# Row scatters of a mixture-of-experts layer spread singly over GpSimd's order

## What is computed

```python
x = x + tanh(g_xattn[0]) * cross_attention(ctx_2048, layernorm(x), mask, mask, ...)   # 8 heads of 16
x_flat = layernorm(x).reshape(-1, 128)
scores = sigmoid(x_flat @ gate.T + bias)                  # 2048 tokens x 9 experts
top_scores, selected = top_k(scores, 2)
top_scores = top_scores / (sum(top_scores) + 1e-20)
for e in range(9):
    h = silu(x_flat @ ew1[e].T) * (x_flat @ ew3[e].T)     # hidden width 352
    out = out + cw[:, e:e + 1] * (h @ ew2[e].T)           # cw: the weight of expert e, or 0
x = x + tanh(g_ffn[0]) * out
```

## Time and profile before

| | |
|---|---|
| timed, median of 3 (lowest, highest) | 231.89 us (231.73, 232.34) |
| profiled execution: span from first to last instruction | 242.9 us |
| profiled execution: its own time around the span | not recorded |
| mean granted TensorE clock of the profiled execution | 0.942 of 2.4 GHz |
| PE, ACT, DVE, POOL busy, share of the span | 83%, 59%, 57%, 51% |
| POOL: x_rows scatters L554, 32 | 32.3 us, 1011 ns mean |
| POOL: y_rows scatters L572, 40 | 39.6 us, 989 ns mean |

### The profile page before, as it was taken

How to read it: one execution, slowest core, us unless ns; L and a number is a source line. 1 busy time by engine, 2 the same in 40 slices (tenths; PEclk the granted TensorE clock), 3 DMA queues, 4 the chain that set the end, 5 groups by cost and what they waited for, 6 DMA issues and landing times.

```text
span 242.9 us, 5743 instructions
## 1 busy us (share of the span) xinstructions
PE 200.9 (83%) x1530; PEld 158.7 (65%) x1531; DVE 139.5 (57%) x511; ACT 143.5 (59%) x400; POOL 123.4 (51%) x209
## 2 busy tenths in 40 slices
PE   8989896999989998977858980599999999999200
PEld 2667653667656665654637870599999999998200
DVE  0397896688897678976643953133444443444035
ACT  0556969788778866875427630356666666665100
POOL 4228735132335784775683477345555555555500
PEclk9999998899999999999988998589999999999955
DMA  5999999987000100011364121112222121260085
GB/s 129 312 331 384 399 402 402 393 304 283 0 4 12 36 33 11 25 34 37 77 167 127 48 66 55 33 46 65 71 67 54 41 58 51 61 213 26 0 299 219
DMA packets 21946, 32.65 MB, mean 134 GB/s; under 512 B 3345, under 2 KB 14742, under 8 KB 21794
## 3 DMA queue, kind: packets, MB, share of 16 engines
q1 hardware_dynamic: 18082, 27.59, 33.7%
q0 software_dynamic: 2304, 4.24, 5.3%
q10 hardware_dynamic: 1536, 0.54, 0.9%
HBM read 15.77 MB, written 17.10 MB: 135 GB/s over the span
## 4 chain that ended last, share of the span: by engine, by line
PE 59%; DVE 14%; issue 10%; DMA 6%; ACT 6%; POOL 2%; ACTq 1%; another core or an unknown queue 0%; POOLq 0%; DVEq 0%; SPq 0%
PE pt_ps L1193 11%; PE score_ps L1155 7%; PE score_ps L1157 5%; PE score_ps L1156 5%; PE pt_ps L1202 5%; PE score_ps L1013 4%; DMA xs<-in_x 4%; PE ps_a L1063 4%; PE ps_b L1118 3%; PE pt_ps L1051 3%; DVE xs L971 2%; PE ps_b L1120 2%; PE ps_a L1172 2%; DMA kheads<-y_rows 2%; DVE less L763 2%
## 5 line engine op out<-in xcount | busy, mean ns | idle before, releaser
L572 POOL DMA_INDIRECT y_rows<-probsT,ids x40 | 39.6, 989 | 32.3 <-ACT probsT L458 24.4
L1193 PE MATMUL pt_ps<-w,probsT 128*128 x234 | 34.7, 287 | 9.6 <-issue 9.2
L1193 PEld LDWEIGHTS pt_ps<-w,probsT 128*128 128x128 f32 x234 | 32.3, 201 | 10.7 <-issue 10.1
L390 ACT ACTIVATE probs<-score_ps,less 128x128 f32<-128x128 f32 x128 | 37.5, 405 | 0.4 <-DVE less L763 0.4
L554 POOL DMA_INDIRECT x_rows<-stage,slot x32 | 32.3, 1011 | 8.8 <-issue 8.8
L914 DVE TENSOR_TENSOR xg_low<-ps_a,xg_high 128x128 fp32r<-128x128 f32 x40 | 11.7, 291 | 43.5 <-ACT xg_high L443 37.0
L458 ACT ACTIVATE probsT<-pt_ps,xg 128x128 f32<-128x128 f32 x39 | 14.3, 367 | 33.5 <-PE pt_ps L1193 27.4
L1155 PE MATMUL score_ps<-w_high,xg_low 128*128 x80 | 30.2, 377 | 0.2
L921 DVE TENSOR_TENSOR probs<-probs,score_ps 128x352 f32<-128x352 f32 x40 | 20.8, 520 | 14.7 <-PE score_ps L1157 5.7
L1156 PE MATMUL score_ps<-w_low,xg_high 128*128 x80 | 26.5, 331 | 0.0
L1157 PE MATMUL score_ps<-w_high,xg_high 128*128 x80 | 26.5, 331 | 0.0
(11 more groups left out here) (152 smaller groups left out, 415.2 us busy)
## 6 DMA issues: line engine op xcount, KB each, us to landing
x_rows<-pads SPq DMA_DIRECT2D x1, 9945.0 KB, 36.5
w_low<-in_w13T SPq DMA_DIRECT2D x3, 1056.0 KB, 10.8
xg<-x_rows SPq DMA_DIRECT2D x40, 65.0 KB, 1.8
ctx_r<-in_ctxT SPq DMA_DIRECT2D x4, 512.0 KB, 8.7
w<-in_w2T SPq DMA_DIRECT2D x1, 1728.0 KB, 9.0
kheads<-y_rows SPq DMA_DIRECT2D x3, 512.0 KB, 4.9
mask_b<-in_mask SPq DMA_DIRECT2D x4, 256.0 KB, 9.0
out<-xs SPq DMA_DIRECT2D x1, 1024.0 KB
```

Source lines behind the costliest of these rows:

```text
L390: last = nc.scalar.activation(probs[:, r % 2, h, :], score_ps[:, r % 2, h, :], ACT.Exp, bias=less[:, r % 2, h:h + 1])
L572: pool.indirect_dma_start(y_rows[:, :], bass.IndirectOffsetOnAxis(ap=ids[:, r:r + 1], axis=0), yt[:, r, :], None, bounds_check=last_row, o ...
L1193: last = nc.tensor.matmul(into[:, 0:D], hidT[:, q3, c, :], w2[:, bass.ds(e3, 1), c, :].rearrange("p o d -> p (o d)"), start=(c == 0), stop ...
```

## The change

It moves scatters; their number and size stay.

- In attention, a group's four batches go out in four steps, one a step: group 0 in steps 9 to 12, group 1 in steps 13 to 16. Of a batch's two scatters the first stands between `rstd2_of` and `keep`, the second at the step's end; `v_cur` moves from the step's start to behind `keep`.
- Behind the last step, batches 0 and 1 of group 2 stand singly between the norms of batches 14 and 15. Batches 2 and 3, and all of group 3 (now in one row behind tile 3), are `paced`: each scatter waits until the last but one has landed.
- Each scatter place has a semaphore of its own, counted to 16 a group; SyncE waits for 8 of them instead of 4 before a row of tile loads, `weigh` too, and `norm2` for 2 instead of 1.

```diff
-        st_rows = [sem(f"st_rows{n}") for n in range(UN)]
+        st_rows = [sem(f"st_rows{n}") for n in range(2 * UN)]
...
-        st_last = [sem(f"st_last{n}") for n in range(UN)]
+        st_last = [sem(f"st_last{n}") for n in range(2 * UN)]
...
                 sp.wait_ge(rows_known, n + 1)
-                for p in range(UN):
-                    sp.wait_ge(st_rows[p], (NG - len(EARLY) + n) * 32)
+                for row in st_rows:
+                    sp.wait_ge(row, (NG - len(EARLY) + n) * 16)
...
             sp.wait_ge(rows_known, len(TILES))
-            for p in range(UN):
-                sp.wait_ge(st_last[p], 32)
+            for row in st_last:
+                sp.wait_ge(row, 16)
...
             def step(k, r, i):
+                group, place = divmod(k - 2 * UN - 1, UN)
+                if on(k, 3):
+                    rstd2_of(k - 3)
+                if group >= 0:
+                    scatter(group, place, 0)
+                if on(k, 3):
+                    keep(k - 3)
                 if on(k, 0):
 
                     if after(k, UN):
                         pool.wait_ge(pv, k - UN + 1)
                     nc.gpsimd.tensor_tensor(v_cur[:, r, :, 0:HD + 1], vals[:, k, :, :], factors[:, k:k + 1, :].to_broadcast([P, H, HD + 1]), ALU.mult).then_inc(v_set, 1)
-                if on(k, 3):
-                    rstd2_of(k - 3)
-                for p in range(UN):
-                    if routed(k, r, 2 * UN + 1 + min(p, 2)) is not None:
-                        scatter(routed(k, r, 2 * UN + 1 + min(p, 2)), p)
-                if on(k, 3):
-                    keep(k - 3)
+                if group >= 0:
+                    scatter(group, place, 1)
...
-            def scatter(g, p):
+            def scatter(g, p, c):
...
+            def paced(g, p):
+
+                for c in range(2):
+                    if p >= 1 and g < NG - 1:
+                        pool.wait_ge(st_rows[2 * p - 2 + c], g * 16 + 16)
+                    elif p >= 1:
+                        pool.wait_ge(st_last[2 * p - 2 + c], 16)
+                    scatter(g, p, c)
+
             rstd2_of(NB - 2)
-            scatter(NG - 2, 0)
+            scatter(NG - 2, 0, 0)
             keep(NB - 2)
-            scatter(NG - 2, 1)
+            scatter(NG - 2, 0, 1)
             rstd2_of(NB - 1)
-            scatter(NG - 2, 2)
+            scatter(NG - 2, 1, 0)
             keep(NB - 1)
-            scatter(NG - 2, 3)
+            scatter(NG - 2, 1, 1)
+            paced(NG - 2, 2)
+            paced(NG - 2, 3)
             for k in range(NT):
                 tile(k, k % TR)
-                if k in (3, 4):
-                    for p in range(2):
-                        scatter(NG - 1, 2 * (k - 3) + p)
+                if k == 3:
+                    for p in range(UN):
+                        paced(NG - 1, p)
...
-                for p in range(UN):
+                for row in st_rows:
                     if g >= 2:
-                        dve.wait_ge(st_rows[p], (g - 1) * 32)
+                        dve.wait_ge(row, (g - 1) * 16)
...
                 if b >= 2 * UN:
-                    dve.wait_ge(st_rows[place], (b // UN - 1) * 32)
+                    dve.wait_ge(st_rows[2 * place], (b // UN - 1) * 16)
+                    dve.wait_ge(st_rows[2 * place + 1], (b // UN - 1) * 16)
```

More of the change, by code:

```diff
@@ L552, in scatter @@
                 pool.wait_ge(kept, g * UN + p + 1)
-                for c in range(2):
-                    pool.indirect_dma_start(x_rows[:, :], bass.IndirectOffsetOnAxis(ap=slot[:, par, c, p:p + 1], axis=0), stage[:, par, c, p, :], None,
-                                            bounds_check=last_slot, oob_is_err=False).then_inc(st_rows[p] if g < NG - 1 else st_last[p], 16)
+                pool.indirect_dma_start(x_rows[:, :], bass.IndirectOffsetOnAxis(ap=slot[:, par, c, p:p + 1], axis=0), stage[:, par, c, p, :], None,
+                                        bounds_check=last_slot, oob_is_err=False).then_inc((st_rows if g < NG - 1 else st_last)[2 * p + c], 16)
             pool.wait_ge(v_done, NG + 1)
```

## The result

The changed kernel takes **232.51 us** (median of 20 runs, 230.82 to 235.62); the kernel before takes 230.89 us on the same chip (20 runs, 228.91 to 232.34). The ratio is 1.0068 [1.0041, 1.0095]: 1.6 us slower, where +1.2 was forecast.

What follows compares the result with a forecast made beforehand. PE was taken to bound the expert tile loop, at 2.07 us a tile. Terms -0.1 + 2.1 - 0.8 = +1.2 us, added to the 231.9 us median, gave 233.1 us; the 8-in-10 range was 229.4 to 235.0.

Steps and rivals of the forecast that it cites:

- (b): Group 1's last scatter moves to step 16, making tile 0's load 2.0 to 3.2 us late; 2.1 taken.
- (c): Batch 15's rstd on GpSimd stands behind two scatters, not four: gives back 0 to 1.44 us; 0.8 taken.
- (a): Attention steps: step 11 holds two scatters instead of four, freeing the next rstd; gain 0 to 0.8 us, 0.1 taken.
- (d): Pacing of ten scatters in groups 2 and 3: 4 to 5 us delay, hidden by 7 us of room before tile 8.
- (e): Group 3 in one row behind tile 3: starts as before, ends up to 1.5 us earlier; costs nothing.
- (f): Added semaphore waits on VectorE and SyncE: 0.03 us each, under 0.3 together; 0.0 in the sum.
- the hole: PE's gap at 145 us in the profile, about 12.3 us lost: recording cost, absent from timed runs; no gain from closing it.
- Rival 1: PE's delays are real in timed runs and single scatters remove them: 4.9 us gain less 1.2, 228.2 us; chance 0.24.
- Rival 2: Nothing reaches the end: (a) and (c) at their upper ends cancel (b)'s 2.1 us; 231.8 us; chance 0.17.
- Rival 3: Pacing bites beside the store: landings over 4 us, tile 16's load becomes the gate; 236 us and more; chance 0.05.

Runs made afterwards that it cites:

- e2: Changed kernel, pacing kept, with both scatters of group 1's last batch back at the end of step 15: median 230.45 us, ratio 0.993.
- e3: Kernel before with only the two scatters of group 1's last batch moved from step 15 to the end of step 16: 233.5 us, ratio 1.0144.
- c1: Kernel before, unchanged, profiled and timed again: 230.29 us, ratio 0.9993, span 230.0.
- e1: Changed kernel without the waits for the last but one scatter's landing, order kept: 230.75 us, ratio 1.0061 to the kernel before.
- c2: Changed kernel, unchanged, run again on another chip: 242.93 us, ratio 1.0022 to the kernel before.
- e4: Changed kernel with the attention order of the kernel before; tail and pacing kept: 243.5 us, ratio 0.9901 to the kernel before.
- e9: e4 repeated on another chip (attention order of before, changed tail and pacing): 242.7 us, ratio 1.0014 to the kernel before.
- e8: e5 repeated on another chip (changed kernel, no pacing, group 1's last batch at end of step 15): 240.72 us, ratio 0.9945 to the kernel before.
- e10: e8 with group 3's batches behind tiles 3, 4, 5 and 6, y scatters between: 240.66 us, ratio 0.9875 to the kernel before.
- e5: Changed kernel without pacing and with group 1's last batch at the end of step 15: 243.22 us, ratio 0.9905 to the kernel before.
- e7: Changed kernel with the 1 MB store of the residual behind the loads of tiles 8 to 15: 243.8 us, ratio 0.9978 to the kernel before.

## Why the prediction came out as it did

**(b) The deciding term, right in mechanism and size.** 2.1 us was taken, out of 2.0 to 3.2. Step 15 to tile 0 measures +2.10. The load comes 9.41 us after step 15's first scatter, where at least 9.3 had been named. e2 removes the wait and is level with the kernel before; e3 lengthens it and costs more. This is shown. That the size is so exact is in part luck: counted from step 15's first score matmul the last scatter ends 2.5 us later than in c1 (9.21 against 6.69), not 2.0, and the load follows it by 2.40 us, not by c1's 2.86.

**(c) The give-back: there, but its cause and size are not settled.** The rstd of batch 15 starts directly behind its variance (2.47 us of wait on VectorE's L822), and PE's idle time before batch 15's second half is gone: 1.01 in c1, none in the changed kernel.

```profile
124.75 0.33 PE L1123 MATMUL ps_b<-cst,stage 128*128 128x128 f32 x1
```

But e3 shows both signs without single scatters behind the last step. So what the prediction took as a mere limit (that (b) makes the variance late by itself) is enough to make them; that the two scatters fewer add to it is not shown. From tile 0 to tile 3 PE needs 8.14 us instead of c1's 8.86, so -0.7 against the -0.8 taken; from tile 0 to tile 7 it is 19.71 against 21.98, so -2.3, and -1.2, -1.2 and -1.8 in e1, e2 and e3. Part of that is a stretch at the 1.2 GHz level in c1: from tile 3 to tile 4 it needs 4.10 us where the changed kernel, e1, e2 and e3 need 2.46 to 2.52.

**(a) Spreading in attention, right within a fraction.** Step 8 to step 15 on PE takes 33.79 us in the changed kernel and 34.04 in e3, which has the order of before in these steps: -0.25, where -0.1 was taken from 0 to -0.8. (c1 shows 35.33, with a stretch at the 1.2 GHz level in it that e3 lacks.) The gain lies where it was looked for, from step 11's first score matmul to step 13's: 10.30 against 10.63 in c1 and 10.64 in e3. The scatters themselves take 0.969 to 1.230 us beside their new neighbours.

**(d) "Hidden": this step failed, in size and in cover.** The prediction took 0 in quiet and 0.5 beside the store, for two to four scatters. The first paced scatter alone waits 3.65 us, then 0.68 and 1.96 follow. And in group 3, with the store long issued, two wait 0.83 and 2.23:

```profile
133.70 0.97 POOL L555 DMA_INDIRECT x_rows<-stage,slot  x1 [0.68 <-DMA x_rows<-stage,slot]
...
136.63 0.97 POOL L555 DMA_INDIRECT x_rows<-stage,slot  x1 [1.96 <-DMA x_rows<-stage,slot]
...
146.97 0.97 POOL L555 DMA_INDIRECT x_rows<-stage,slot  x1 [0.83 <-DMA x_rows<-stage,slot]
...
151.44 0.97 POOL L555 DMA_INDIRECT x_rows<-stage,slot  x1 [2.23 <-DMA x_rows<-stage,slot]
```

Tile 8's load is issued at 139.88 (131.95 in the earlier trace rows) and PE uses it at 141.75, 1.79 us late. The 7 us of room were read correctly; the delay was put at 4 to 5 and came to 7.9 in the load's issue (of which 2 are (b)'s). Behind the wait PE runs at the 1.2 GHz level for a stretch, and the window 140 to 145 shows a granted clock of 0.74:

```profile
140.00:145.00 5.00, 3.19 (x13) 3.00 (x14) 3.42 (x16) 1.20 (x4) 3.96 (x6) 0.74 0.36 93
```

From tile 7 to tile 8 the changed kernel needs 4.07 us against 2.42 in e1, which has no pacing, and from tile 8 to tile 16 18.93 against 18.26: 2.3 us in that profile. In the timed runs it is smaller: e1 is 0.8 us slower than the kernel before by the medians and 1.4 by the ratio, the changed kernel 1.6 beside its own runs of the kernel before, so 0.2 to 0.8 is left for the pacing, which I can't resolve. The other four profiles with pacing and the store (c2, e2, e4, e9) show no wait for tile 8's load. So the pacing has used up the room and bites in some executions.

**(e) "Nothing" was right in the time and wrong in the reading.** Group 3 was to start as before and to end up to 1.5 us earlier. It starts at 143.90 and ends at 156.31; in c1 it is 139.84 and 151.24. Tile 16's load is issued at 158.73 (153.74 in c1) and PE uses it at 160.68, 1.95 us later; for tiles 0 and 8, on which PE waited, it was 1.85 and 1.87. So about 0.1 us of room is left there, an estimate from these rows.

```profile
158.73 10.24 SPq L308 DMA_DIRECT2D xg<-x_rows  x8
```

**(f)** No run shows the term of 0.03 us for each wait; what the profiles show in its place is that no engine's wait of note is put down to these semaphores. It was not tried by itself.

**The sum** was +1.2. The stretches of the changed profile against c1 (and e3 for the attention steps) give -0.25 + 2.10 - 2.27 (tiles 0 to 7) + 1.77 (tile 7 to 8: 4.07 against 2.30) + 0.72 (tiles 8 to 16: 18.93 against 18.21) = +2.1, and the timed runs +1.6. That it came out close owes something to luck: (d) was left out, and (c) was taken too small. e1, in which (d) is absent, is the fairer test of the sum: +0.8 to +1.4.

**What the prediction said of the hole was wrong.** It took the 11 us between span and median for recording cost, on the premise that a timed run holds all that the span holds. The Trainium skill (NOTIFIC — the notification-queue block, Overflow: three behaviours, one of which stalls the engine) says that the internal path of the records holds back its producers when it is full; no run here shows it at work. c1 was recorded on chip A and has no hole (span 230.0). On chips B and C every execution of the kernel before is longer, none below 239.82 us, and the span of 242.9 lies among theirs (238.0 to 244.5). So the hole goes with the chip, and the profile of before most likely came from another chip than its three times; the record doesn't name it. The conclusion, that the timed runs beside the result have no hole, was right all the same, and so was adding differences to the median.

**Rival 1** (single scatters remove PE's delays): its time, 228.2, came nowhere, but its mechanism is real on chips B and C and small on A. From step 11's first score matmul to step 13's, where four scatters in a row stood, PE needs 11.63 to 11.66 us in the three profiles that have the order of before and the hole (before, e4, e9) and 10.29 or 10.30 in all nine with the scatters spread; on A the order of before takes 10.63 and 10.64. On chip C, e9 and then c2:

```profile
82.70 0.38 PE L1032 MATMUL score_ps<-bias_b,share 64*128 64x512 bf16 x2
...
94.36 0.38 PE L1032 MATMUL score_ps<-bias_b,share 64*128 64x512 bf16 x2
```

```profile
84.08 0.38 PE L1033 MATMUL score_ps<-bias_b,share 64*128 64x512 bf16 x2
...
94.38 0.38 PE L1033 MATMUL score_ps<-bias_b,share 64*128 64x512 bf16 x2
```

So the spreading is worth 1.4 us there and 0.3 on A, and (b), with 13.39 us from step 15 to tile 0 in c2 against 11.77 in e9, takes 1.6 back: the changed kernel is level on C. e8 and e10, without (b) and the pacing, are 1.7 and 1.8 us faster than the kernel before by the medians, which is about what the spreading is worth; e5 on B is 0.8 faster. **Rival 2** (nothing reaches the end) is refuted by e2 and e3. **Rival 3** (pacing bites) named landings over 4 us, tile 16's load and 236 us. The landing did take 4.8 us from the scatter's end (130.77 - 0.30 - 125.66, an estimate from GpSimd's rows); PE waited at tile 8, at tile 16 it came within 0.1 us, and the time stayed far from 236.

## What to carry to other kernels

A wait that another engine's first load hangs on is worth more than an even spacing of the work ahead of it: find the last producer of each gate (here group 1's last scatter for tile 0) and keep it where it was while spreading the rest. A wait for a landing must be priced with what else moves at that time: a landing put at 1.4 us in quiet took 4.8 beside a 1 MB store, and the scatter that waited for it stood for 3.65. And before a gap in a profile is explained or explained away, compare span plus some 1.8 us with the timed runs; if they disagree by per cents, profile and times may be of different chips, and a change that pays on one may cost on another.

## What the runs showed that I had not expected

- One program takes 229.92 us on one chip and 243.98 or 242.43 on two others, in all of 29, 33 and 31 executions. The difference lies mostly between tiles 0 and 16, where ScalarE waits for PE's results (single waits of up to 6 us). Eight scatters in a row (e8), eight paced ones (c2) and pairs between y scatters (e10) all have it on chip C; eight in a row without any wait for landings have none of it on A (e1: 41.4 us from tile 0 to tile 16). So the packing of the scatters is not sufficient, nor is the 1 MB store needed (e7). What does it, and why on some chips, stays open.
- A scatter takes 0.97 us behind another scatter, 0.98 behind the copy, 1.02 behind v_cur and 1.09 to 1.23 behind the rstd, as the rows of the changed kernel's timeline show. The mean over 32 is 1.029 us, where c1 has 1.012:

```profile
L555 POOL DMA_INDIRECT x_rows<-stage,slot x32 | 32.9, 1029 | 15.7 <-DMA x_rows<-stage,slot 10.0
```

- The same kernel's executions on one chip differ by some 3 us with the mean granted clock: c1 has 228.43 to 230.29 us at 0.959 to 0.963 in six runs, 230.29 and 230.92 at 0.951 and 0.952, and 231.37 to 233.09 at 0.942 to 0.950. A change of 1 us is only seen over many runs.
